# A message-passing layer on one core: a third stage order with single buffers, longer rings, clears four in flight and gathers that wait for the pair before

## The reference, cut to what matters

```python
h   = x @ W_in2f                                   # 50000 x 256
Wij = (ssp(rbf @ Wf1 + bf1) @ Wf2 + bf2) * dist_cut  # ssp(v) = softplus(v) - log 2; rbf is 50000 x 64
x_ij = h[idx_j] * Wij                              # idx_j = dst
m   = segment_sum(x_ij, idx_i, 50000)              # idx_i = src
m   = ssp(m @ Wo1 + bo1) @ Wo2 + bo2
out = layernorm(x + (x + m))                       # over the 256 features
```

## Time and profile before

| | us |
|---|---|
| median of 3 runs (lowest to highest) | 1863.84 (1859.76 to 1867.15) |
| the profiled execution | 1858.28 |
| its span, first to last instruction | 1856.5 |

### The profile page before, as it was taken

One profiled execution on the slowest core, in us unless ns is written; L12 is line 12 of the kernel. 1 busy time (PEld: TensorE's weight loads), 2 busy tenths in 40 slices (PEclk: granted clock), 3 DMA queues, 4 the chain that ended last, 5 costly groups with the idle time before them and its releaser, 6 DMA issues. The chain is left out here.

```text
span 1856.5 us, 36676 instructions
## 1 busy us (share of the span) xinstructions
PE 1697.3 (91%) x11376; PEld 1532.2 (83%) x11376; DVE 1489.3 (80%) x3750; ACT 1492.9 (80%) x2945; POOL 1441.4 (78%) x1385
## 2 busy tenths in 40 slices
PE   3499899999999999999999998889976999999995
PEld 2378788888888888888888887778866999999995
DVE  2477788787888888888888786777765999999996
ACT  2477788778888788888888786776756999999996
POOL 7422488888887888878888888888754999999997
PEclk9699999999999999999999998999998999999998
DMA  9799866656566665666665666665675999999994
GB/s 354 251 356 372 266 123 112 126 112 125 115 125 122 112 123 114 124 125 112 125 120 116 119 122 113 114 118 108 116 185 170 333 363 362 360 360 364 357 366 174
DMA packets 177341, 363.47 MB, mean 196 GB/s; under 512 B 25622, under 2 KB 76264, under 8 KB 177148
## 3 DMA queue, kind: packets, MB, share of 16 engines
q1 hardware_dynamic: 101128, 257.75, 39.8%
q0 software_dynamic: 75136, 102.45, 32.4%
q10 hardware_dynamic: 884, 0.92, 0.2%
HBM read 206.90 MB, written 154.12 MB: 194 GB/s over the span
## 5 line engine op out<-in xcount | busy, mean ns | idle before, releaser
L354 POOL DMA_INDIRECT acc<-sums,src_ix x392 | 637.2, 1626 | 141.6 <-issue 116.0
L341 POOL DMA_INDIRECT xg<-in_x,dst_t x392 | 401.4, 1024 | 215.6 <-issue 114.6
L780 DVE SCALAR_TENSOR_TENSOR m_l<-pair,wgt_t,m_h 128x256 fp32r<-128x256 f32 x392 | 171.6, 479 | 230.5 <-ACT m_h L621 206.6
L385 POOL TENSOR_SCALAR sums<-sums,neg_mean,rstd 128x256 f32<-128x256 f32 x392 | 283.2, 733 | 10.2
L495 PE MATMUL pair<-m_h,same 128*128 128x256 f32 (+1 forms) x980 | 244.8, 285 | 30.4 <-ACT sums L628 21.9
L621 ACT ACTIVATE m_h<-pair,wgt_t 128x256 fp32r<-128x256 f32 x392 | 165.0, 475 | 99.5 <-PE pair L409 57.6
L495 PE MATMUL pair<-m_l,same 128*128 128x256 f32 (+1 forms) x980 | 241.8, 281 | 0.0
L409 PE MATMUL pair<-wo_h,msg_h 128*128 128x256 f32 (+1 forms) x784 | 230.9, 295 | 6.0 <-DVE m_l L780 5.2
L495 PEld LDWEIGHTS pair<-m_h,same 128*128 128x128 f32 (+1 forms) x980 | 185.1, 189 | 52.2 <-issue 34.9
L576 ACT ACTIVATE zs<-pair,bf 128x512 f32<-128x512 f32 x196 | 124.1, 685 | 125.8 <-PE pair L433 99.5
L409 PE MATMUL pair<-wo_h,msg_l 128*128 128x256 f32 (+1 forms) x784 | 222.0, 283 | 0.0
(11 more groups left out here) (97 smaller groups left out, 5249.8 us busy)
## 6 DMA issues: line engine op xcount, KB each, us to landing
acc<-fill SPq DMA_DIRECT2D x197, 256.0 KB
xg<-in_x SPq DMA_DIRECT2D x97, 512.0 KB, 6.4
sums<-acc SPq DMA_DIRECT2D x97, 512.0 KB, 6.8
out<-sums SPq DMA_DIRECT2D x97, 512.0 KB, 4.7
attr<-in_edge_attr SPq DMA_DIRECT2D x196, 128.0 KB
srcb<-in_src_rows SPq DMA_DIRECT2D x98, 256.0 KB
xg<-in_x,dst_t POOLq DMA_INDIRECT x392
acc<-sums,src_ix POOLq DMA_INDIRECT x392
```

The costliest lines, as they stand in the source:

```text
L341: pool.indirect_dma_start(xg[0:g.p, g.xs, r], None, t["x"], bass.IndirectOffsetOnAxis(ap=dst_t[0:g.p, r, g.n:g.n + 1], axis=0)).then_inc(x ...
L354: pool.indirect_dma_start(acc, bass.IndirectOffsetOnAxis(ap=src_ix[g.slot][0:g.p, r:r + 1], axis=0), sums[0:g.p, g.slot, r], None, compute ...
L385: last = pool.tensor_scalar(normed[0:g.p, g.n % NRING, r], res[0:g.p, u, r], neg_mean[0:g.p, u, r:r + 1], rstd[0:g.p, u, r:r + 1], ALU.add ...
L780: dve.scalar_tensor_tensor(out=m_l[0:g.p, r], in0=bank[6][0:g.p, k * D:(k + 1) * D], scalar=col(wgt_t, r, g), in1=m_h[0:g.p, r].bitcast(F3 ...
```

## The change

- **Buffers.** `x_h`, `x_l`, `ssp_h`, `ssp_l` and `same` lose their second half; `ssp` and `msg` are no longer tiles: `softplus` and `message` write back into their PSUM banks (2 + h and 5), and the splits read from there. So `filter1` now waits for `sspl_sb` and `w_of` for `msgl_sb`, and the splits of x wait for the `h_of` of the group before (`h_ps`, g.n * H).
- **Rings.** RING goes from 12 to 14, XRING from 11 to 17, AHEAD from 23 to 30.
- **Order.** PE, ACT and DVE get new lists, with lags of 0 to 3 where there were 0 to 4; `compare` is split into four stages.
- **Head.** At most four clears are in flight: clear c waits for the landing of clear c - 4. There are still 198; the three for the spare rows now come last. The wait for the first gather is gone. The gathers of groups 2 to 29 wait for the landing of those two groups back.
- **x for the second half.** `fetch_x` moves into SP's loop, right behind the transposes that free its slot, for 16 groups, and one behind the loop: 17 where there were 11.
- **Placement.** The big tiles that DMAs touch (`sums`, `xg`, `attr`, `srcb`, `fill`) are declared first, all small ones last or inside `sums` and `to_spare`.

```diff
-RING = 12
-XRING = 11
+RING = 14
+XRING = 17
-AHEAD = 23
-EARLY_CLEARS = 8
+AHEAD = 30
+IN_FLIGHT = 4
...
+                    wait(sp, cleared[c % IN_FLIGHT], c // IN_FLIGHT * 16)
...
-            clear_to(EARLY_CLEARS)
-            sp.wait_ge(xg_in[0], 16 * R)
             clear_to(FIRST_CLEARS)
...
+                if G - XRING <= n - 2:
+                    fetch_x(group((n - 2) % XRING))
...
+                    if r == 0 and 2 <= g.n < AHEAD:
+                        b = group(g.n - 2)
+                        pool.wait_ge(xg_in[b.xs], xg_count(b))
...
-                wait(pe, ssp_sb, g.n * H)
+                wait(pe, sspl_sb, g.n * H)
...
-                    wait(pe, msg_sb, g.n * H + m)
+                    wait(pe, msgl_sb, g.n * H + m)
...
-            run((w_of(1), 2), (summed(0), 3), (h_of(0), 1), (summed(1), 3), (filter1, 0), (turn_x(0), 0),
-                (out1(0), 2), (turn_x(1), 0), (w_of(0), 1), (h_of(1), 1), (out1(1), 2), before={1: filter_bias})
+            run((w_of(1), 2), (summed(1), 3), (turn_x(0), 0), (turn_x(1), 0), (out1(0), 2), (h_of(0), 1), (filter1, 0),
+                (w_of(0), 1), (out1(1), 2), (h_of(1), 1), (summed(0), 2), before={1: filter_bias})
...
-            run((keep_y(0), 4), (msg_high(1), 3), (ssp_high(0), 2), (ssp_high(1), 2), (keep_h(0), 2), (absolute(0), 1),
-                (absolute(1), 1), (expo(0), 1), (m_high(0), 3), (keep_y(1), 4), (expo(1), 1), (x_high(0), 1), (loga(0), 1),
-                (loga(1), 1), (x_high(1), 1), (keep_h(1), 2), (m_high(1), 3), (a_high, 0), (msg_high(0), 2), before={1: weights})
+            run((x_high(0), 1), (keep_y(0), 3), (x_high(1), 1), (ssp_high(0), 1), (msg_high(1), 2), (ssp_high(1), 1), (keep_y(1), 3),
+                (a_high, 0), (m_high(0), 2), (keep_h(0), 1), (absolute(0), 0), (absolute(1), 0), (expo(0), 0), (expo(1), 0),
+                (loga(0), 0), (loga(1), 0), (msg_high(0), 1), (m_high(1), 2), (keep_h(1), 1), before={1: weights})
...
-            run((m_low(0), 3), (message(0), 2), (x_low(0), 1), (softplus(0), 1), (softplus(1), 1), (x_low(1), 1),
-                (m_low(1), 3), (message(1), 2), (a_low, 0), (msg_low(0), 2), (target, 3), (msg_low(1), 2), (ssp_low(0), 1),
-                (ssp_low(1), 1), (compare, 2), before={1: first_weights, 2: tables, 3: second_weights})
+            run((x_low(0), 1), (message(1), 2), (x_low(1), 1), (msg_low(1), 2), (ssp_low(0), 1), (ssp_low(1), 1), (a_low, 0),
+                (compare(0), 2), (m_low(0), 2), (compare(1), 2), (compare(2), 2), (message(0), 1), (compare(3), 2), (softplus(0), 0),
+                (msg_low(0), 1), (softplus(1), 0), (m_low(1), 2), (target, 2),
+                before={0: biases, 1: first_weights, 2: tables, 3: second_weights})
```

More of the change, by code:

```diff
@@ L304, in store @@
                 sp.dma_start(rows_of(out, g).rearrange("(p r) d -> p (r d)", r=R), normed[0:g.p, u].rearrange("p r d -> p (r d)")).then_inc(stored[u], 16)
-            for n in range(G - XRING, G):
+            for n in range(G - 1, G):
                 fetch_x(group(n % XRING))
@@ L348, in stage @@
                         if g.n == 0:
-                            pool.wait_ge(cleared, 16 * (CLEARS + CLEAR_REST))
+                            for u in range(IN_FLIGHT):
+                                pool.wait_ge(cleared[u], 16 * len(range(u, CLEARS, IN_FLIGHT)))
                         pool.wait_ge(src_ready, g.n + 1)
@@ L449, in stage @@
                     transposed(m, bank[4][:].rearrange("f (r e) -> f r e", r=R)[:, :, 0:g.p], w_in_h, w_in_l,
-                               [x_h[:, g.par, k, :, 0:g.p] for k in range(H)], [x_l[:, g.par, k, :, 0:g.p] for k in range(H)]).then_inc(h_ps, 1)
+                               [x_h[:, k, :, 0:g.p] for k in range(H)], [x_l[:, k, :, 0:g.p] for k in range(H)]).then_inc(h_ps, 1)
                 return stage
@@ L494, in stage @@
                             for m in (m_h, m_l):
-                                last = pe.matmul(o, same[0:g.p, g.par, FROM[a] + b - a, 0:g.p], m[0:g.p, a],
+                                last = pe.matmul(o, same[0:g.p, FROM[a] + b - a, 0:g.p], m[0:g.p, a],
                                                  start=a == 0 and m is m_h, stop=a == b and m is m_l)
@@ L526, in stage @@
                             for sp2, w in ((ssp2_h, wo2_h), (ssp2_h, wo2_l), (ssp2_l, wo2_h)):
-                                last = pe.matmul(o, sp2[:, g.par, h, r, 0:g.p], w[:, h, :], start=False, stop=h == H - 1 and sp2 is ssp2_l)
+                                last = pe.matmul(o, sp2[g.par][:, h, r, 0:g.p], w[:, h, :], start=False, stop=h == H - 1 and sp2 is ssp2_l)
                     last.then_inc(o_ps, 1)
@@ L736, in a_low, with compare, stage @@
                 low(a_l[:, :, 0:g.p], attr[:, g.n % ARING].rearrange("f (r e) -> f r e", r=R)[:, :, 0:g.p], a_h[:, :, 0:g.p], al_sb)
-            def compare(g):
-                dve.wait_ge(srcb_in[g.n % SRING], (g.n // SRING + 1) * 16)
-                wait(dve, y_ps, (g.n - 1) * 2)
-                sources = srcb[0:g.p, g.n % SRING].rearrange("x (r e) -> x r e", r=R)[:, :, 0:g.p]
-                for a in range(R):
-                    dve.scalar_tensor_tensor(out=same[0:g.p, g.par, FROM[a]:FROM[a] + R - a, 0:g.p], in0=sources[:, a:R],
+            def compare(a):
+                def stage(g):
+                    if a == 0:
+                        dve.wait_ge(srcb_in[g.n % SRING], (g.n // SRING + 1) * 16)
+                        wait(dve, y_ps, g.n * 2)
+                    sources = srcb[0:g.p, g.n % SRING].rearrange("x (r e) -> x r e", r=R)[:, :, 0:g.p]
+                    dve.scalar_tensor_tensor(out=same[0:g.p, FROM[a]:FROM[a] + R - a, 0:g.p], in0=sources[:, a:R],
                                              scalar=col(src_t, a, g), in1=later[0:g.p, 0:R - a, 0:g.p], op0=ALU.is_equal, op1=ALU.mult,
                                              accum_out=alike[0:g.p, g.par, a:a + 1]).then_inc(same_ready, 1)
+                return stage
             def target(g):
@@ L770, in stage @@
                     wait(dve, m_ps, g.n * 2)
[L771 removed]
+                    low(msg_l[:, m], bank[5][:].rearrange("f (r e) -> f r e", r=R), msg_h[:, m], msgl_sb)
                 return stage
```

126 lines of the change are left out of this document (62 added, 64 removed).

## The result

| | us |
|---|---|
| the kernel after, median of 4 runs (lowest to highest) | 1904.24 (1898.82 to 1910.01) |
| the kernel before, median of 4 runs | 1862.67 (1859.76 to 1867.15) |
| ratio, 95% interval | 1.0221, 1.0183 to 1.026 |
| the profiled execution of after, its span | 1902.33, 1900.6 |

The change makes the kernel slower by 2.2%, where 1850 us and a range up to 1890 had been forecast. The two profiled executions differ by 1902.33 - 1858.28 = 44.1 us, and four marks say where they lie.

The account below looks back on a forecast made before the run. Bounds before: DMA engines in the head, PE and GpSimd in the long run, ACT in the second half. Last scatter 213 + 85 x 13.46 + 27.9 = 1385.0 against 1396.9; with 2 us more, 14 us gained: 1850 us, range 1808 to 1890.

Parts of the forecast that it names:

- The loop: Long run: a dependency loop through DVE, ACT and PE sums to 13.26 us, taken as 13.46 us a step.
- One sign: Long run: GpSimd should wait for `keep_y` from about the first groups on.
- the term that decides: Long run: the step of 13.46 us, bounds 12.8 and 13.9; 85 steps times 0.1 us is 8.5 us.
- The end: Last split of x to last scatter: 27.9 us, where it was 36.2 us.
- The second half: Start of the second half: earlier fetch of x gains 2 us.
- GpSimd alone at 1344: Long run: at 11.75 us a group GpSimd alone would issue the last scatter at 1344 us, if PE keeps up.
- The head: Start up to group 12: its x split at about 213 us, where it was 223.53; bounds 206 and 224.
- The rival that the head would not change: Head: stalls stay, x of group 12 at 224, 11 us more, 1861 us; chance 0.08.
- Four clears in flight: Head: four clears of 256 KB each, one per 0.87 us including loads, should just do.
- The starved rival: Head: four clears in flight starve the DMA engines, 21 us a step instead of 13.9, median 1920; chance 0.08.
- The landing wait: Head: the gathers' wait for two groups back costs nothing, as eight gathers, 10 us, lie between.
- The alignment of the tiles: Head: new placement might quicken clears by up to a tenth, some 14 us; the sum takes nothing for it.

Follow-up runs that it names:

- e5: Kernel after with `target` moved behind compare(3) in DVE's list: 1864.25 us in one execution; timed again, ratio 1.0139 to the kernel before.
- e6: Kernel before with the gathers ahead spread, even groups waiting for transposes and odd ones for `h_of`: 1865.77 us, one execution.
- e7: Kernel before with three waited memsets ahead of each gather of groups 1 to 10: 1861.54 us, one execution.
- run 28: Not a label: "that run 28 gathers longer" means GpSimd's unbroken run of gathers, 48 long in the kernel before and 76 in the kernel after.
- e2: Kernel after with clears issued as in the kernel before, none waiting for a landing: 1888.59 us, one execution.
- e10: e9 with clears issued as in the kernel before, none held back: 1845.45 us, ratio 0.99 to the kernel before.
- e9: Kernel after, `target` moved, four waited memsets ahead of each gather of groups 1 to 29 replacing the landing wait: 1856.84 us, ratio 0.9949 to the kernel before.
- e4: Kernel after without the gathers' wait for the landing two groups back: 1904.74 us, one execution.
- e14: e10 with the waited memsets kept only up to group 13: 1868.33 us, ratio 1.0016 to the kernel before.
- e13: e10 with two waited memsets instead of four per gather from group 14 on: 1838.19 us, ratio 0.9863 to the kernel before.
- e3: Kernel before with gathers of the head waiting for PE's transposes of the group four back, up to a cap of 8: 1867.19 us, one execution.
- e16: Kernel after with gathers of half a row, 512 bytes instead of 1024, so not the layer's result: 1890.28 us, one execution.

## Why the prediction was wrong

- **The loop: right.** 13.46 us a step was said and 13.45 measured from group 32 to 74, and 1139.9 us from group 12 to 97, where 85 x 13.46 = 1144 was said. The parts fit too: the median step is 13.19 us where the loop's own sum was 13.26, and the mean lies 0.26 above it where 0.2 were given for disturbances. e5 confirms the loop by itself: `target` off it gives 0.28 us a step. One sign failed: GpSimd was to wait for `keep_y` from about the first groups on, and from 1000 to 1300 us it waits 3.4 us for it and 20.7 for `target`. What the prediction named as the term that decides was sized rightly and decided nothing against the head.
- **The end: right.** 27.9 us from the last split of x to the last scatter were said, 28.4 measured.
- **The second half: nearly right.** 2 us less were said, 1.0 more came.
- **GpSimd alone at 1344: not reached**, as the sum had it. The prediction rightly said that PE and GpSimd end together in the kernel before. What it didn't draw from that is what e6 and e7 show: a shorter head alone gains nothing there.
- **The head: wrong by 59 us, and this is the step that failed.** "A shorter queue of clears should take away part of that." x of group 12 was said at 213 and came at 271.7. The rival that the head would not change, at 224, was itself 48 us short. The reading of the earlier trace rows (TensorE stands with nothing to wait for) was right, and the cause given to it, a deep queue of clears, was a guess that no row bore. PE's stall was to shrink and came twice, 25.1 and 26.8 us; the first scatter, whose coming after 225 us was to show the prediction wrong, came at 265.5. One view would have spoken: the timeline of POOL has its first pause at 71.79, right behind x1 at 65.2, and the ring of 17 makes that run 28 gathers longer. I counted those gathers as bytes, 9 us, where they are 36 us of standstill.
- **Four clears in flight: under-priced.** They "should just do"; e2 shows 10.7 us of x12, and 16 us of the time, and where the stall is gone they cost more of the head: 36.0 us of x12 from e10 to e9, 11.4 us of the time. The starved rival said 21 us a step. SP's step in the head went from 13.9 to 15.5 us (149.5 to 257.8 in seven steps), and is 17.9 in e9: the rival priced it too high, but its mechanism is there. The stall hid most of it.
- **The landing wait: free**, as said (e4).
- **The alignment of the tiles: open.** The sum took nothing for it, and no run separates it.

With the head at 271.7 instead of 213 the sum gives 271.7 + 1144.1 + 27.9 = 1443.7, against 1440.0 measured.

## What to carry to other kernels

Where GpSimd issues a long series of indirect transfers ahead of a loop, look in the timeline at whether the other engines' idle time by "issue" begins and ends with that series; if so, try spacing the transfers. Here waited memsets that made it 1.55 to 1.9 us a transfer were worth 30 us of 1868 (e14 to e13), and a longer ring without them made the head worse by 36 us. And before shortening a head, add up what the engine that ends last still has to issue after it: the kernel before gave back nearly all of 20 us (e6, e7), with GpSimd's 676 transfers unchanged. Measure such a head more than once. A mark in the trace for each part of the sum (here four) finds the part that failed at once.

## What the runs showed of the hardware

- Beside unbroken indirect gathers of 128 rows (one per 1.25 us) matmuls of 128x512 start up to 2.8 us apart instead of 0.235 (e14) and complete every 2.8 us (the kernel after), so that completions come up to 53 us late. The DMA engines meanwhile stand at anything from 1.05 down to 0.37. It sets in at the full granted clock (e3) and goes on at half of it, and ACT's instructions keep their times. At 1.9 us a gather (e10) and, from 107 us on, at 1.55 (e13) PE had no gap of 4 us or more from 25 us to the first scatter.
- The stall sets in 7 to 25 us after the run begins and ends near its end (99.9 and 101.2, 64.0 and 65.2, 157 and 155 to 165). It isn't complete: e3 let 27 matmuls through between 150 and 160 us.
- It isn't certain: one execution of five of the same kernel went without it, 26 us faster, with gathers every 1.28 us.
- A gather of half the bytes takes GpSimd as long: one per 1.25 us in e16 too.
